# A four-batch transformer decoder: context keys and half the context values projected in earlier stages

## The reference

```python
x = x + L0_attn(ln(x))            # landmark attention, 64 landmarks
x = x + L0_xattn(ln(x), ctx)      # causal attention + context attention, 16 heads of 16, then @ Wp + bp
x = x + L0_ffn(ln(x))             # linear layer with weights and inputs rounded to fp6
x = x + L1_attn(ln(x))            # hyperbolic causal attention
x = x + L1_xattn(ln(x), ctx)      # twice attention (16 heads of 32) and a GELU block
x = x + L1_ffn(ln(x))             # 8 experts, best 2 of each row
```

```python
q = hidden @ Wq + bq; k = hidden @ Wk + bk; v = hidden @ Wv + bv    # landmark attention
q = softmax(q, -1); k = softmax(k, -1)
k_landmarks = k.reshape(B, 64, 8, D).mean(2)
output = (q @ k_landmarks^T) @ ((k_landmarks @ k^T) @ (k * v))

qc = heads(x @ Wcq + bcq)                  # context attention: 512 queries,
kc = heads(ctx @ Wck + bck)                # 1024 keys
vc = heads(ctx @ Wcv + bcv)
y  = y + softmax(qc @ kc^T / 4) @ vc
```

## Time and profile before

| what | value |
|---|---|
| median of 3 runs | 4127.66 us (4120.45 to 4134.79) |
| profiled execution | 4113.2 us, span 4111.5 us |
| TensorE busy | 3402.3 us, 83% |
| VectorE busy | 2072.7 us, 50% |
| ScalarE busy | 1644.0 us, 40% |
| mean granted TensorE clock | 0.921 |

### The profile page before, as it was taken

The page is one execution under the profiler, slowest core; times in us unless marked ns, Lnnn a source line. Parts: engine busy times, 40 slices in busy tenths (PEclk is TensorE's granted clock), DMA queues, the critical chain, the costliest instruction groups (busy, mean ns, idle before and its releaser), DMA issues. The chain is left out here.

```text
span 4111.5 us, 56764 instructions
## 1 busy us (share of the span) xinstructions
PE 3402.3 (83%) x21854; PEld 1868.5 (45%) x21854; DVE 2072.7 (50%) x4215; ACT 1644.0 (40%) x2361; POOL 919.0 (22%) x961
## 2 busy tenths in 40 slices
PE   6897688898887788988887888988886888946997
PEld 4325445245324535254235534264244552435886
DVE  4564655634555664634655565534746556430111
ACT  2343833332354742433446542424437433411221
POOL 1201822011103722012106521012018320130111
PEclk9999799998898999999897999999897999958998
DMA  3203012111103012011211021012130112134554
GB/s 102 67 12 77 1 44 75 33 37 45 47 12 77 1 44 87 20 42 39 58 54 24 9 77 50 17 42 66 31 77 1 41 60 51 32 121 153 178 173 153
DMA packets 227197, 239.82 MB, mean 58 GB/s; under 512 B 95542, under 2 KB 193956, under 8 KB 224612
## 3 DMA queue, kind: packets, MB, share of 16 engines
q1 hardware_dynamic: 220560, 216.65, 18.3%
q0 software_dynamic: 3744, 10.26, 0.7%
q10 hardware_dynamic: 2612, 9.15, 0.6%
HBM read 167.24 MB, written 68.76 MB: 57 GB/s over the span
## 5 line engine op out<-in xcount | busy, mean ns | idle before, releaser
L858 ACT ACTIVATE prob<-psum 128x1024 f32<-128x1024 f32 x384 | 372.2, 1021 | 513.5 <-PE psum L776 513.5
L1199 ACT ACTIVATE prob<-psum 128x1024 f32<-128x1024 f32 (+3 forms) x384 | 331.2, 914 | 424.7 <-PE psum L1116 424.7
L904 DVE TENSOR_REDUCE scr<-psum 128x1 f32<-128x512 f32 x576 | 369.4, 686 | 199.2 <-PE psum L763 195.3
L1238 DVE TENSOR_REDUCE stats<-psum 128x1 f32<-128x512 f32 (+3 forms) x576 | 334.2, 620 | 162.7 <-PE psum L1104 157.3
L394 PE MATMUL psum<-ident 128*128 128x128 f32 x2008 | 254.3, 284 | 14.6 <-PEq L1828 9.6
L394 PEld LDWEIGHTS psum<-ident 128*128 128x128 f32 x2008 | 243.1, 199 | 29.4 <-issue 28.5
L1116 PE MATMUL psum<-stack 32*128 32x512 f32 (+3 forms) x1536 | 209.9, 617 | 49.7 <-ACT prob L1199 41.8
L773 PE MATMUL psum<-stack 32*128 32x512 f32 x1536 | 226.6, 660 | 15.2 <-ACT prob L858 10.4
L806 PE MATMUL psum<-prob,ones_f 128*32 128x512 f32 x1536 | 203.8, 598 | 0.0
L1131 PE MATMUL psum<-prob,vbig 128*32 128x512 f32 (+3 forms) x1536 | 194.5, 580 | 4.2 <-ACT prob L1199 4.2
L2740 PE MATMUL psum<-xgT,ew 128*128 128x256 f32 x736 | 167.6, 386 | 18.0 <-DVE xgT L2788 18.0
(11 more groups left out here) (474 smaller groups left out, 6426.9 us busy)
## 6 DMA issues: line engine op xcount, KB each, us to landing
ew<-in_L_ffn_W SPq DMA_DIRECT2D x46, 1024.0 KB, 7.5
stack<-q_terms SPq DMA_DIRECT2D x144, 128.0 KB, 2.6
w_mlp<-in_L_xattn_a_li_w SPq DMA_DIRECT2D x16, 1024.0 KB, 6.9
q_terms<-parts SPq DMA_DIRECT2D x96, 128.0 KB, 2.4
stack<-k_terms SPq DMA_DIRECT2D x72, 128.0 KB, 3.0
w_mlp<-k_terms SPq DMA_DIRECT2D x36, 256.0 KB, 4.6
w_mlp<-a_terms SPq DMA_DIRECT2D x36, 256.0 KB, 4.7
a_keys<-stack SPq DMA_DIRECT2D x4, 2048.0 KB, 6.3
```

The costliest lines, as they stand in the source:

```text
L858: act.activation(prob[:, i % 4, :, :], psum[:, 2 * p:2 * p + 2, :], ACT.Exp, scale=scale).then_inc(exped, 1)
L904: dve.tensor_reduce(found[:, c:c + 1], ring(i), AX.X, ALU.max).then_inc(freed, 1)
L1199: act.activation(prob[:, i % 4, :, q0:T], psum[:, 2 * p:2 * p + 2, q0:T], ACT.Exp, scale=scale).then_inc(exped, 1)
L1238: dve.tensor_reduce(found[:, c:c + 1], ring(i)[:, 0:keys_of(t)], AX.X, ALU.max).then_inc(freed, 1)
```

## The change

The keys of the context attention are projected by TensorE at the beginning of the landmark attention, in place of 32 of 36 warm-ups, into `w_mlp`, which is free there and stays so until the context attention ends. ScalarE takes four of the eight pieces and VectorE four. The landmark attention's transposes are regrouped in halves, so that ScalarE copies them in two pieces. The second norm projects the last four tiles of context values in place of six of its 14 warm-ups. "Bca" is called with `ready=2`: its jobs are four queries and two value jobs, and ScalarE cuts the ready keys to "high" from SBUF instead of PSUM. The key terms move from `w_mlp` to `stack`. In the start stage seven row loads go from SP to ScalarE's queue, ScalarE issues its small loads first, and VectorE's quantising goes ahead of four small copies.

```diff
@@ start
-            for n, dst in R.items():
+            for n, dst in early_rows:            # the first 4 of 11
                 late(dst, spread(dram[n]))
@@ start, scalar
-            load_context(act, slice(0, 1))
-            for i, n in enumerate("qkv"):
-                act.dma_start(bA[:, i * C:(i + 1) * C], spread(dram[f"L0_attn_b{n}"])).then_inc(bias_in, 16)
             act.wait_ge(blanked, 1)
...
+            for i, n in enumerate("qkv"):
+                act.dma_start(bA[:, i * C:(i + 1) * C], spread(dram[f"L0_attn_b{n}"])).then_inc(bias_in, 16)
+            load_context(act, slice(0, 1))
             act.wait_ge(raw_in, 16 * len(heads))
...
+            for n, dst in late_rows:
+                act.dma_start(dst, spread(dram[n])).then_inc(loads, 16)
+                n_late[0] += 1
@@ narrow_heads
+        if ready:
+            first = [("q", 0, 0)]
+            jobs = first + [("q", 1, 0)] + of_tiles(0, 1) + [("q", 2, 0), ("q", 3, 0)] + of_tiles(1, twos - ready)
+        n_early = len(jobs)
...
+        splits = [(kind, g, h) for kind, g, h in jobs if kind != "v" and g]
+        if ready:
+            splits = splits[:1] + [("k", g, h) for g in range(1, HG) for h in range(halves)] + splits[1:]
...
-                        pe.wait_ge(taken, 2 + h if b0 else len(jobs))
+                        pe.wait_ge(taken, n_early if not b0 else 1 if ready else 2 + h)
...
+                def keys_to_high(g):
+                    if g >= 3:
+                        act.wait_ge(stored, 64 * (g - 2))
+                    for h in range(halves):
+                        act.copy(high("k", g, h), whole("k", g, h)).then_inc(keys_high, 1)
...
+                        if ready and i + 1 == n_early:
+                            keys_to_high(2)
+                            keys_to_high(3)
...
+                    if ready and g == 1:
+                        keys_to_high(1)
@@ landmark_attention, vector (between the maxima and the wait for the exponentials)
+            for i in BY_DVE:                     # parts 2 to 5
+                dve.wait_ge(keyed, i + 1)
+                dve.tensor_scalar(key_part(i), psum[:, i, :], key_bias(i), None, ALU.add).then_inc(keys_by_dve, 1)
@@ landmark_attention, scalar
+            take_key(0)
+            take_key(1)
             act.wait_ge(maxed, 1)
...
-            act.wait_ge(turned, 1)
-            act.copy(qkT, psum[:, 0:4, :]).then_inc(copied, 1)
+            take_key(6)
+            take_key(7)
+            for h in range(2):
+                act.wait_ge(turned, h + 1)
+                act.copy(qkT[:, :, h * 2 * P:(h + 1) * 2 * P],
+                         psum[:, 2 * h:2 * h + 2, :].rearrange("p b (c n) -> p (b c) n", n=2 * P)).then_inc(copied, 1)
@@ landmark_attention, tensor
-            e.keep_running(pe, 36, 7)
+            for i, (g, h) in enumerate(parts_of_keys):
+                pe.matmul(psum[:, i, :], e.wBck[:, 0, g * P:(g + 1) * P], e.cT[:, 0, h * BANK:(h + 1) * BANK],
+                          start=True, stop=True).then_inc(keyed, 1)
+            pe.wait_ge(keys_by_act, 2)
+            e.keep_running(pe, 4, 0)
...
@@ standard_attention
-    e.norm("n2", x, e.xh, turns=[(xT, None, None)], idle=(14, 5))
+    e.norm("n2", x, e.xh, turns=[(xT, None, None)], idle=(8, 5), beside=(late_values, take_late_values))
...
-                   work[:, 0:2048].rearrange("p (g n) -> p g n", g=HG), work[:, 2048:6144].rearrange("p (g n) -> p g n", g=HG),
+                   work[:, 0:2048].rearrange("p (g n) -> p g n", g=HG), e.context_keys,
                    stack[:, 12288:16384].rearrange("p (s j n) -> p s j n", s=2, j=J),
-                   e.q_stack.rearrange("p (s j n) -> p s j n", s=2, j=J), add=e.colB[:, 0, :])
+                   stack[:, 4096:12288].rearrange("p (s j n) -> p s j n", s=2, j=J), add=e.colB[:, 0, :], ready=ready)
```

More of the change, by code:

```diff
@@ L394, in keep_running, with norm @@
             pe.matmul(psum[:, bank, at:at + P], ident[:, :], ident[:, :], start=True, stop=True, skip_group_check=True)
-    def norm(tag, src, dst=None, turns=(), gain=None, n=QT, width=C, also=None, first=None, more=(), idle=(0, 0)):
+    def norm(tag, src, dst=None, turns=(), gain=None, n=QT, width=C, also=None, first=None, more=(), idle=(0, 0),
+             beside=None):
         kts = width // P
@@ L470, in _ @@
                         return
+                    if beside is not None:
+                        beside[0](pe, beside_summed)
                     dst = passes[-1][1]
@@ L969, in narrow_heads @@
         then_event = []
-        for kind, _g, _h in jobs[len(first):]:
+        for kind, _g, _h in jobs[len(first):n_early]:
             since += (wq if kind == "q" else wk if kind == "k" else wv).shape[1]
@@ L1143, in _ @@
                 queue = list(before)
-                for i in range(len(first), len(jobs)):
+                for i in range(len(first), n_early):
                     project(i)
@@ L1204, in _ @@
                 pool.memset(pad[:, :, :], 0.0).then_inc(pads_zero, 1)
-                for i, (kind, g, h) in enumerate(jobs):
-                    if kind == "v" or g == 0:
-                        continue
-                    pool.wait_ge(taken, i + 1)
+                for kind, g, h in splits:
+                    if ready and kind == "k":
+                        pool.wait_ge(keys_high, (g - 1) * halves + h + 1)
+                    else:
+                        pool.wait_ge(taken, jobs.index((kind, g, h)) + 1)
                     pool.tensor_tensor(middle(kind, g, h), whole(kind, g, h), high(kind, g, h),
@@ L1935, in standard_attention, with late_values, take_late_values @@
     x, xT, V, Vc = e.x, e.xT, e.V, e.Vc
-    e.norm("n2", x, e.xh, turns=[(xT, None, None)], idle=(14, 5))
-    work, stack, colQK = e.work, e.stack, e.colQK
+    work, stack, colQK, psum = e.work, e.stack, e.colQK, e.psum
+    ready = 2
+    def late_values(pe, summed):
+        for a in range(ready):
+            for i in range(2):
+                last = pe.matmul(psum[:, 4 + a, i * C:(i + 1) * C], e.cT[:, 0, (CT - 2 * ready + 2 * a + i) * P:(CT - 2 * ready + 2 * a + i + 1) * P],
+                                 e.wBcv[:, 0, :], start=True, stop=True)
+            last.then_inc(summed, 1)
+    def take_late_values(act, summed):
+        for a in range(ready):
+            act.wait_ge(summed, a + 1)
+            for i in range(2):
+                act.copy(Vc[:, CT - 2 * ready + 2 * a + i, :].rearrange("p (h w) -> p h w", w=W)[:, :, 0:D16],
+                         psum[:, 4 + a, i * C:(i + 1) * C].rearrange("p (h w) -> p h w", w=D16))
+    e.norm("n2", x, e.xh, turns=[(xT, None, None)], idle=(8, 5), beside=(late_values, take_late_values))
     e.narrow_heads("Ba", (e.wBq, colQK[:, 0, :], xT), (e.wBk, colQK[:, 1, :], xT), e.wBv, V, T,
```

80 lines of the change are left out of this document (54 added, 26 removed).

## The result

The changed kernel took 4072.97 us (median of 4 runs, 4065.65 to 4079.66); the kernel before 4129.8 us beside it (4120.45 to 4134.79). The ratio is 0.9865, with a 95% interval of 0.9837 to 0.9892. It is faster, and by more than the forecast of 4099 and its range from 4075. Gains of 45 to 51 us lie in both intervals; 28.4 were forecast. The profiled execution took 4068.3 us (span 4066.5), against 4113.2 (4111.5).

What follows compares the result with a forecast made beforehand. TensorE was busiest (83%), but the context attention's quads were bound by its projections and VectorE's reduces in turn. Context attention 22.4, landmark attention 0, second norm 0, start 6.0: 28.4 us off the median 4127.66 gives 4099; range 4075 to 4114.

Steps and rivals of the forecast that it cites:

- Quads: Context attention, first matmul to last reduce: 26.8 us instead of 32.4; 5.6 us less per batch, 22.4 in four.
- The chain around quad 3: Context attention: quad 3 waits until ScalarE has taken all six jobs, q3's after group 1's stores; its reduce starts at 183.0.
- The prediction's last sentence: Forecast wrong if quad 3 waits for ScalarE, the landmark attention grows, or the slow stretch changes length; no size.
- Start: Start stage: seven row loads leave SP's queue, so the stage ends sooner; 6.0 us, once, bounds 0 to 6.9.
- The rule of the Trainium skill: Start stage: another issuing engine saves only sequencer time, so the start gives 0 instead of 6.0; chance 0.12.
- the same slow stretch behind it: Context attention, behind the quads: the low-clock stretch stays equally long at the same program place; counted as nothing.
- rival (a): Clock behind the quads: one slow step less or more, 2.7 us per batch, 10.8 in all; chance 0.14 each way.
- Landmark attention: Key jobs replace warm-ups, 0.3 us gained; taken as 0, bounds 1.5 gained and 1.0 lost per batch.

Runs made afterwards that it cites:

- after_again: The changed kernel itself, unedited, measured a second time against the kernel before: 4081 us, ratio 0.9896.
- warm2_before: Kernel before plus matmuls computing nothing in the context attention, 2 calls ahead of each of quads 4 to 7, 10 behind the last: 4100 us, 0.9937 of before.
- warm2_after: Changed kernel plus matmuls computing nothing in the context attention, 2 calls ahead of each of quads 4 to 7, 10 behind the last: 4056 us, 0.9836 of before.
- gaps_only: Changed kernel plus 2 calls of matmuls computing nothing ahead of each of quads 4 to 7, none behind the last: 4074 us, 0.9883 of before.
- keys_in_landmark: Kernel before with only the changed landmark attention; keys projected there go unused and are projected again later: 4119 us, 0.9995 of before.
- values_in_norm: Kernel before with only the changed second norm; its two value jobs are done again in the context attention: 4110 us, 0.9984 of before.
- start_alone: Kernel before with only the three edits of the start stage: 4111 us, 0.9978 of before.
- tail_only: Changed kernel plus 10 calls of matmuls computing nothing behind the last quad only: 4056 us, 0.9841 of before.
- values_back: Changed kernel with the second norm's two value jobs back in the context attention behind q3, and 14 warm-ups again: 4094 us, 0.992 of before.
- warm_after: Changed kernel plus matmuls computing nothing in the context attention, 8 calls ahead of each of quads 4 to 7, 36 behind the last: 4091 us, 0.9925 of before.

## Why the forecast was right about the edits and wrong about the clock

The excess of one profile over the forecast, 45.0 - 28.4 = 16.6 us, is made up so: the quads 1.3, the start 2.4, the part behind the turn 6.8, the stages up to the second norm 3.0, the stages behind the context attention 6.1, less 3.0 in the self attention.

**Quads: right.** 26.5 us from first matmul to last reduce (26.8 forecast), 23.7 us in four batches for 22.4. The chain around quad 3 went as written, with small shifts: group 1's loads were issued at 169.15, 12.2 us after the first matmul (12.3 forecast), and quad 3 waited for ScalarE's taking of the last value job. (The prediction's last sentence counts such a wait as a sign of being wrong, though its own chain has it.)

**Start: right.** 7.0 us alone against 6.0; 8.4 in this profile, an early one. The rule of the Trainium skill, "DMA: Bandwidth & Descriptors", section "Issuing engines are not separate DMA queues", would have given 0. The runs differ from it: the issuing itself was what ended the stage, since SP's queue was held up for 6.74 us by four loads, and a second queue took that away. ScalarE's queue can be held up too: its last four row loads took 2.0 us in the changed kernel's profile and 5.05 in after_again, where the next stage's first work came 3.6 us later.

**The step that failed** is "the same slow stretch behind it", counted as nothing and left to rival (a) with a chance of 0.14. The forecast had seen that bare quads leave TensorE half idle from early on. It took from this that the clock would be low "at the same place of the program" for two steps. In fact it falls 7.6 us ahead of the turn, inside the part that VectorE bounds, where before it fell 3.0 us ahead; and it lasts 17.1 us instead of 23.9. So 9.4 us of slow work are left behind the turn in three batches instead of 20.9 (17.1 in the fourth). This is worth 13.3 us in this profile from the turn to the second group, 6.8 us when the later short stretches are counted, and 3.2 in the second execution. warm2_before and warm2_after show the price: with the clock up, the first part is 36.5 us in both kernels. That the earlier start of the stretch is due to the gaps between the bare quads is shown by gaps_only. Why it is shorter isn't shown, and the second execution (24 us in its first batch) says that chance has a part in it. Rival (a) had the sign and the mechanism; its 10.8 us were one whole step of 2.7 a batch, where the first part gave 4.0, 4.0, 1.3 and 4.0 and the whole behind the turn 1.8, 1.9, 0.5 and 2.5. The forecast also had no term for what the clock does in stages that the change doesn't touch (below).

**Landmark attention: mis-sized at 0.** It is 3.3 us in four batches by keys_in_landmark's one profile and 5.6 by the averages above, within the bounds given (up to 1.5 a batch). The reason given was wrong: the keys aren't faster than the warm-up (from the stage's first matmul to the first product 13.75 us with them and 13.80 before, in most batches); what follows them is, since its clock stays up.

**Left out:** 6.1 us in stages that the change doesn't touch. They are the clock too: 6.6 of them in one stage, which took 52.2 us in each batch before and 50.6 after, less 0.5 elsewhere. At 657 us before it opened with 32 matmuls of 8.83 us; the same took 7.21 us after, since the granted clock there was 0.52 and 0.63 in the windows 658 to 660 and 660 to 662 before, and 1.00 after. keys_in_landmark and values_in_norm, whose edits lie in stages far ahead, have 50.6 us there too; start_alone has 52.2. Against this the self attention lost 3.0 us.

**Still open:** these terms add up to the 45 us of the two profiles. The medians of the first comparison differ by 57, those of the second by 39 (43 by its ratio); the interval of either is some 10 us to each side, so which of the two is nearer isn't settled. The median lies 2 us outside the stated range, and at least that much of the miss can be chance. Nor is settled what sets how long a low clock lasts once it has begun: 7 to 44 us were seen around the turn for nearly the same program.

## What to carry to other kernels

Where a change makes TensorE idle for a moment, cost the moment and also the clock that follows it, and ask where the slow stretch will lie: under another engine's bound it is free, behind it each step pays (7.75 instead of 5.06 us here). Two and a half microseconds of filler in the last idle gap gave 25 us over four batches; a filler of 36 calls for 10 there, and 8 for 2 between the quads, lost more than it gave. And compare profiles by parts: an edit's gain in its own stage can be half hidden by low-clock stretches that moved elsewhere. Where one engine's queue ends a start stage, look at how long its issues are held up before believing that the data are the bound.

## What the runs showed of the hardware that wasn't expected

- In the changed kernel TensorE's clock fell to 1.2 GHz at 176.4 us, in the bare quads, when the engine had been busy for 4.55 of the last 8.40 us and no wait had been longer than 1.66 us. The Trainium skill, "TensorE: Matmul & The Clock Gate", section "A second HAM failure mode: psum-queue depth-cycling", tells of such short idle times between groups of matmuls; the trace agrees, since filling them moved the fall from 19 to 26 us of the stage. The trace of before can't show this: there the clock fell at 197.3 us, 0.8 us into the idle time behind the last quad.
- The low clock lasted 7 us (tail_only), 17 (the changed kernel), 24 (before), and 31 to 44 (values_back), with the same instructions behind it.
- Untouched stages hundreds of microseconds later were 1.65 us a batch shorter or longer (50.57 or 52.22 us), in the same direction in nearly all batches of a kernel. The self attention, the same code in all, took from 339.9 (before) to 354.4 us (warm_after) in four batches.
- Issuing four 128-partition row loads took 6.74 us on SP in the kernel before and 2.0 (the changed kernel) to 5.05 us (after_again) on ScalarE. What was in flight differed; that this is the reason isn't shown by an experiment of its own.
